# The second weight of a projection stage loaded at its start, into a buffer of its own, instead of at its end

## What is computed

```python
v = out32 @ W_write.T                  # projection of all tokens
# chunked scan, equal to: reads[t] = sum over s < t of gamma^(t-1-s) * <xn[t], xn[s-1]> v[s]
return out + alpha * (reads @ W_read.T)
...
h = jax.nn.relu(x @ Wq1.T + b1)        # Wq1, Wq2: ternary weights
out = h @ Wq2.T + b2
...
x = x + _L1_attn_ref(xn, ...) + _L1_ffn_ref(xn, ...)
```

## Time and profile before

| | |
|---|---|
| Time, two runs | 1594.59 and 1623.49 us, median 1609.04 |
| Profiled execution | 1598.28 us |
| Its span on core 7, the slowest | 1596.7 us (first to last instruction) |
| Spans of the eight cores | 1573.7 to 1596.7 us |
| PE busy | 1242.3 us, 78% of the span |
| ACT, DVE busy | 475.1 us (30%), 418.8 us (26%) |
| Granted TensorE clock, mean over the span | 0.91 |

### The profile page before, as it was taken

How to read it: one execution, slowest core, us unless ns; L and a number is a source line. 1 busy time by engine, 2 the same in 40 slices (tenths; PEclk the granted TensorE clock), 3 DMA queues, 4 the chain that set the end, 5 groups by cost and what they waited for, 6 DMA issues and landing times. The chain is left out here.

```text
span 1596.7 us, 15373 instructions; the slowest of 8 cores (1573.7 to 1596.7 us)
## 1 busy us (share of the span) xinstructions
PE 1242.3 (78%) x5440; PEld 535.6 (34%) x5440; DVE 418.8 (26%) x704; ACT 475.1 (30%) x550; POOL 139.0 (9%) x184
## 2 busy tenths in 40 slices
PE   0275289996796777665469499979997999889997
PEld 0121034442332223222124144434443444334443
DVE  1497435003223324333175200020002200031000
ACT  0564033334425526536023141013202140031400
POOL 2331100000101111212100000000000000000000
PEclk9988589997898888887789799989998999989999
DMA  8795942003326637556650742343335152241423
GB/s 194 110 171 89 141 74 49 1 0 103 117 72 210 184 120 232 176 206 203 135 89 1 211 144 94 105 184 115 97 122 195 33 152 80 101 163 53 132 103 108
DMA packets 74202, 194.42 MB, mean 122 GB/s; under 512 B 8272, under 2 KB 16496, under 8 KB 69776
## 3 DMA queue, kind: packets, MB, share of 16 engines
q0 software_dynamic: 37072, 105.34, 27.4%
q1 hardware_dynamic: 37056, 88.09, 17.3%
HBM read 195.57 MB, written 33.56 MB: 143 GB/s over the span
## 5 line engine op out<-in xcount | busy, mean ns | idle before, releaser
L1181 PE MATMUL pb<-bigA,wqA 128*128 128x512 bf16 x1024 | 226.2, 379 | 0.0
L1141 PE MATMUL pb<-xn,xbf 128*128 128x512 bf16 x1024 | 222.5, 380 | 0.0
L1124 PE MATMUL pb<-stm,bigB 128*128 128x512 bf16 x640 | 145.4, 389 | 34.6 <-DVE xa_bf L997 28.3
L1082 ACT ACTIVATE bigA<-pb,cstF 128x512 bf16<-128x512 f32 x128 | 99.6, 778 | 219.7 <-PE pb L1141 219.7
L1163 PE MATMUL pb<-rt,projW 128*128 128x512 bf16 x512 | 126.1, 391 | 43.9 <-DVE rt L1002 39.4
L1032 DVE SCALAR_TENSOR_TENSOR xf<-pb,cstF,xf 128x512 f32<-128x512 f32 x32 | 24.0, 750 | 479.5 <-PE pb L1181 479.5
L1141 PEld LDWEIGHTS pb<-xn,xbf 128*128 128x128 bf16 x1024 | 100.2, 98 | 121.7 <-issue 0.2
L1181 PEld LDWEIGHTS pb<-bigA,wqA 128*128 128x128 bf16 x1024 | 100.2, 98 | 120.8
L1111 PE MATMUL pb<-xn 128*128 128x512 bf16 x320 | 79.7, 416 | 51.5 <-PEq L922 29.2
L667 PE MATMUL pb<-projW,xn 128*128 128x512 bf16 x512 | 112.3, 381 | 0.0
L1124 PEld LDWEIGHTS pb<-stm,bigB 128*128 128x128 bf16 x640 | 63.1, 100 | 116.9 <-issue 47.2
(11 more groups left out here) (127 smaller groups left out, 1092.4 us busy)
## 6 DMA issues: line engine op xcount, KB each, us to landing
wqA<-W2qS POOLq DMA_DIRECT2D x32, 1024.0 KB, 5.2
xbf<-W1qS SPq DMA_DIRECT2D x128, 256.0 KB, 2.5
xbf<-W2T SPq DMA_DIRECT2D x26, 512.0 KB, 4.2
bigA<-W2T POOLq DMA_DIRECT2D x32, 256.0 KB, 9.3
bigA<-W1T POOLq DMA_DIRECT2D x16, 512.0 KB, 9.8
xf<-xT SPq DMA_DIRECT2D x4, 2048.0 KB, 8.7
x1S<-xf POOLq DMA_DIRECT2D x4, 2048.0 KB, 8.2
stm<-W1T SPq DMA_DIRECT2D x16, 512.0 KB, 5.4
```

Of the source, the lines that this page charges most:

```text
L1082: got = si(s.activation(bigA[:, fc * 512:(fc + 1) * 512], pb[fc % 2][:, :], AF.Relu, bias=biasL[:, 48 + fc:49 + fc], scale=sc[:, C_Q4:C_Q4 ...
L1124: got = ti(t.matmul(bank[:, :], bigB[:, i * 1024 + ec * 128: i * 1024 + (ec + 1) * 128], stm[:, i * 512:(i + 1) * 512], start=(n == 0), st ...
L1141: got = ti(t.matmul(bank[:, :], xbf[:, (fc % 4) * 1024 + dc * 128: (fc % 4) * 1024 + (dc + 1) * 128], xn[:, p0:p0 + TS], start=(dc == 0), ...
L1181: got = ti(t.matmul(bank[:, :], wqA[:, (dc % 2) * 4096 + fc * 128: (dc % 2) * 4096 + (fc + 1) * 128], bigA[:, fc * 512:(fc + 1) * 512], st ...
```

## The change

`WwrT` goes to the first half of `bigA` instead of to `projW`. With `projW` free, POOL issues the loads of `WrdT` (on semaphore sDn) and of `nm` (on sDl) straight behind the load of `WwrT`, at the start of the block; the wait for PE's last `vtm` is gone, and at the block's end POOL waits for sDn and sDl. The `vtm` matmuls of layer 1 read `bigA`. Layer 0 is as before.

```diff
@@ POOL, ln_proj @@
                     q_w[0] = qgD(g, projW[:, :], full_mat_src(Wk))
                 else:
-                    q_w[0] = qgD(g, projW[:, :], full_mat_src(WwrT))
+                    q_w[0] = qgD(g, bigA[:, 0:8192], full_mat_src(WwrT))
+                    q_w[1] = qnD(g, projW[:, :], full_mat_src(WrdT))
+                    q_w[2] = qlD(g, nm[:, :], nmB)
                 for j in (1, 2, 3):
@@ POOL, end of ln_proj @@
                 else:
-                    g.wait_ge(sT, t_tok[pseq[-1]])
-                    q_w[1] = qgD(g, projW[:, :], full_mat_src(WrdT))
-                    q_w[2] = qgD(g, nm[:, :], nmB)
-                    g.wait_ge(sQg, q_w[2])
+                    g.wait_ge(sDn, q_w[1])
+                    g.wait_ge(sDl, q_w[2])
@@ PE, vtm @@
                         if layer == 0:
                             t.wait_ge(sQg, q_w[1])
+                            wsrc = projW
                         else:
                             t.wait_ge(sQg, q_w[0])
+                            wsrc = bigA
...
-                                projW[:, dc * 1024 + et * 512: dc * 1024 + (et + 1) * 512],
+                                wsrc[:, dc * 1024 + et * 512: dc * 1024 + (et + 1) * 512],
```

## The result

The changed kernel takes 1573.31 us in the median; the kernel before, on the same chips, 1594.8 us. In a few executions of either kernel half of the cores showed a lower granted clock and the time was longer (1672.28 us in one of the changed kernel), and the ratios leave these out. The ratio is 0.9867, with a 95% interval of 0.985 to 0.9884: 1.3% faster, less than the 2% that the prediction took as the least a measurement of this kernel can tell, yet with an interval clear of 1. The forecast was 1576 us and 22.1 us of gain; measured are 0.0133 x 1594.8 = 21.2 us.

What follows compares the result with a forecast made beforehand. PE, busy 78% of the span, was taken to bound the kernel through its idle or low-clock stretches. Removing 20.5 us of pause, gaining 2.1 us of clock and charging 0.5 us took 1598.28 to 1576 us, range 1567 to 1598.

Steps and rivals of the forecast that it cites:

- What is removed: End of layer-1 projection: PE's idle wait for the late WrdT and nm loads goes, tile 0 starts 20.5 us earlier.
- The clock: Start of tile 0: after a 1.8 us pause PE keeps 2.4 GHz, first 32 matmuls gain 2.1 us.
- One sum on the way: Clock estimate: 128 matmuls after 5.04 us of idleness took 29.59 us, called 1.8 us over four times 7.07.
- The slack of 1.2 us ahead of the feed-forward weights: In tile 0 the first feed-forward weight lands at +13.8, PE asks at +15.0, so the load stays hidden.
- a sign that the prediction had listed under wrong: A wait of PE at the first feed-forward matmul would show the forecast wrong.
- What is added: Start of layer-1 projection: in-order queue delays tile 2 to 827.5, needed by 828.3; 0.5 us charged.
- a second sign of being wrong: A DMA wait of DVE at line 694 before tile 2 would show the forecast wrong.
- the first rival: Layer-1 projection and tile 0: tile 2 comes 4.6 us late and PE stays at 1.2 GHz; 1582.4 us, chance 0.10.
- The sum: Core 7: 20.5 + 2.1 - 0.5 = 22.1 us gone, from 1598.28 to 1576.2 us; core 7 still sets the time.
- The descriptor rival: Layer-1 projection: later transfers get no descriptors while DVE works, tile 2 26.2 us late; 1601.9 us, chance 0.04.
- the third rival: Barrier before tile 0: another engine or semaphore holds it, half the tail at risk; 1588 us, chance 0.08.

Runs made afterwards that it cites:

- the run that separates it: Kernel with only nm loaded late at the block's end, plus 29 unread PE matmuls beside that load; ratio 0.9915 to the kernel before.
- The two tries: Unread PE matmuls beside late loads: 82 added to the kernel before, ratio 1.0003; 29 added to the changed kernel with nm loaded late, 0.9915.
- the second execution: Another profiled execution of the changed kernel, nothing altered; mean 99.70 us from block start to last projection matmul, 693.35 us from tile 0 to the end.
- the run with 2 MB more: Changed kernel plus one more load of WrdT into bigA's unused second half, behind nm and ahead of tile 2; ratio 0.9973, median 1588.4 us.

## Why the prediction was right

*What is removed.* Right: 20.5 us predicted for the slowest core, 20.56 us between the pauses of the two slowest cores. ACT's DRAIN came last, and the barrier cost 1.03 us for 1.06. The mean core gained less, 17.5 us, because WrdT took 13.3 us to land on some cores and 17.6 on core 7; the prediction had this spread for core 3 only. That core 7 would go on setting the time was wrong: in the profiled execution it is core 4, and which core is slowest changes from execution to execution in either kernel.

*The clock.* Right as a mechanism, with 7.09 us for 7.07, and right in size: 2.1 us predicted, 2.2 us between the means, 2.4 us in the run that separates it (1.35 us between the two slowest cores). The two tries to show it in the time of the slowest core failed. One sum on the way was off: 29.59 us are 1.3 us over four times 7.07, not 1.8; the forecast doesn't use it. The slack of 1.2 us ahead of the feed-forward weights was all but used up: on two cores of the second execution PE waited 0.3 to 0.4 us there, a sign that the prediction had listed under wrong.

*What is added.* The mechanism held: order of issue, and tile 2 pays. The size was low. WrdT took 12.9 us behind WwrT where I took 12.2 from layer 0, nm 3.3 for 2.5, tile 2 5.9 for 6.6, and WwrT itself 27.5 for 26.1. The last is no effect of the change: on core 4 WwrT took 27.5 us in the kernel before as well, and the 26.1 us were core 7's. Tile 2 landed 51.3 us after the block's first issue, not 49.2, and was needed at 50.0. So core 4 lost about 1.5 us and the mean core 0.5 to 0.8, for the 0.5 charged. Here a second sign of being wrong came true: DVE waited for tile 2, 1.96 us on core 4, which reached it 1.9 us later in the block than core 7 had before, not within 1 us. It means that the late tile of the first rival did occur, without the loss of clock and at a third of that rival's 4.6 us.

*The sum.* Between the two slowest cores it is 20.6 + 1.35 - 1.65 = 20.3 us, for 22.1 predicted, and the whole kernel gained 21.2 us. That the total lies within 1 us of the forecast is in part luck, as the clock gave less on these cores and tile 2 cost more than I had charged, and half of this shortfall of 1.8 us is made up by 0.9 us that these stretches don't account for. The forecast of 1576 us also started from 1598.28 us, 3.5 us above the median of before.

*The rivals.* The descriptor rival is refuted by the run with 2 MB more, and by the changed kernel itself, in which WrdT, nm and tile 2 landed while DVE worked. The Trainium skill's rule ("SBUF — State Buffer", its note on DVE blocking DMAs) speaks of DVE operations in a two-port mode; no run here shows a transfer held up beside this block's DVE work. For the third rival I argued that only DRAINs of 0.6 us stand at the barrier. That reading was wrong though the number was right, and the forecast was lucky in it: a DRAIN of POOL lasts until its youngest DMA has landed. In the changed kernel it took 11.3 us, and it cost nothing only because tile 3, the youngest load, had landed 45 us before ACT's DRAIN.

*What stays open.* The 4.7 us by which the changed kernel's profiled execution was ahead at the block's start, and why loads land later on the cores that start the block late, weren't looked into.

## What to carry to other kernels

A second buffer is worth what the transfer costs at the place where nothing else runs, plus the clock that PE loses in the pause; price both from the pause in the trace, and then ask what the moved load is put ahead of in its queue. At a block's end look at what the last DRAIN covers: in this kernel a DMA issued late by POOL held the barrier until it had landed, whether or not the program waited for it, and the same store from SP didn't. A pause that is removed at a barrier can come back at the next wait: here layer 1 kept all of its gain and layer 0 gave back over half at PE's wait for DVE.

## What the runs showed of the hardware

- POOL's DRAIN ended 0.3 to 0.4 us after its last DMA had landed (13.63 us for a landing of 13.3, 17.48 for 17.1, and 11.30 us where tile 3 was in flight); SP's took 0.13 us with a store in flight for 7.4 us.
- Ahead of tile 0, PE kept 2.4 GHz over every pause of up to 1.90 us, and lost it in every one of 3.42 us or more. Between them it went both ways: 32 matmuls in 8.69 us after 2.49 us, in 7.09 us after 2.76 us.
- The loads on POOL's queue landed in their order of issue in every trace shown here, and the DMA share was 1.07 to 1.10 beside a DVE busy for two thirds of the time.
